# Five routing stages of a one-core transformer kernel: token numbers as two 16-bit digits, one row gather ahead of the stage barrier

## What is computed

```
layer 0: 8 experts, top 2, hidden 352 (and a shared expert)   weights = softmax over experts
layer 1: 8 experts, top 1, hidden 1024, biases
layer 2: two groups of 32 experts, top 2, hidden 128, added
layer 3: 32 experts, top 1, hidden 256, at most 80 tokens each (tokens past that are dropped)
ffn(x)[t] = sum over the chosen experts e of  w[t,e] * (silu(x[t] @ gate_e) * (x[t] @ up_e)) @ down_e
```

## Time and profile before

| | before |
|---|---|
| median of 3 runs | 2540.61 us (2532.79 to 2540.71) |
| the profiled execution | 2542.26 us, its span 2540.5 us |
| busy PE / PE weight load | 2044.3 us (80%) / 1660.4 us (65%) |
| busy DVE / ACT / POOL | 1307.0 us (51%) / 842.3 us (33%) / 737.2 us (29%) |
| granted TensorE clock, mean | 0.88 of full speed |
| DMA | 280.78 MB, mean 111 GB/s |

### The profile page before, as it was taken

How to read it: one execution, slowest core, us unless ns; L and a number is a source line. 1 busy time by engine, 2 the same in 40 slices (tenths; PEclk the granted TensorE clock), 3 DMA queues, 4 the chain that set the end, 5 groups by cost and what they waited for, 6 DMA issues and landing times. The chain is left out here.

```text
span 2540.5 us, 41393 instructions
## 1 busy us (share of the span) xinstructions
PE 2044.3 (80%) x13605; PEld 1660.4 (65%) x13605; DVE 1307.0 (51%) x3958; ACT 842.3 (33%) x2000; POOL 737.2 (29%) x928
## 2 busy tenths in 40 slices
PE   6869979992799999998589748995895953887694
PEld 5657746661698989987589735664684832554594
DVE  3532225524688888886400156765346445675423
ACT  4613313422133333333333223453341421345321
POOL 1022100005344444454111122310546743231132
PEclk9969989985899999999699969995796986898797
DMA  2052130002211111100199534426576653442384
GB/s 79 9 207 63 53 114 13 1 1 77 84 35 42 43 44 43 38 20 7 60 354 335 206 111 123 134 71 233 158 146 235 176 107 101 117 118 57 141 310 155
DMA packets 142732, 280.78 MB, mean 111 GB/s; under 512 B 20160, under 2 KB 99008, under 8 KB 138432
## 3 DMA queue, kind: packets, MB, share of 16 engines
q1 hardware_dynamic: 125824, 232.49, 27.3%
q0 software_dynamic: 16704, 45.64, 7.7%
HBM read 218.94 MB, written 56.62 MB: 108 GB/s over the span
## 5 line engine op out<-in xcount | busy, mean ns | idle before, releaser
L1956 PE MATMUL heads_ps_c<-heads_band,heads_sT 128*128 128x129 f32 x3072 | 368.9, 277 | 14.4 <-DVE heads_band L2175 13.4
L1956 PEld LDWEIGHTS heads_ps_c<-heads_band,heads_sT 128*128 128x128 f32 x3072 | 355.0, 192 | 24.7 <-issue 22.9
L2112 POOL TENSOR_SCALAR heads_band<-heads_shifts,heads_taps 128x130 f32<-128x130 f32 x384 | 251.1, 668 | 254.5 <-PE heads_ps_c L1956 250.3
L506 POOL DMA_INDIRECT weights_xg<-xn_rows,token_of x197 | 189.9, 964 | 449.3 <-DVE token_of L686 192.8
L2175 DVE SCALAR_TENSOR_TENSOR heads_band<-heads_shifts,heads_taps,heads_band 128x130 f32<-128x130 f32 x768 | 226.7, 351 | 18.4 <-POOL heads_band L2112 13.7
L2049 ACT ACTIVATE heads_probs<-heads_mixes,heads_least 128x256 f32<-128x256 f32 x256 | 116.1, 500 | 343.8 <-DVE heads_least L2188 343.8
L1697 DVE TENSOR_REDUCE heads_negmax<-heads_ps_m 128x2 f32<-128x512 f32 x256 | 169.6, 688 | 83.6 <-PE heads_ps_m L1553 81.3
L1654 ACT ACTIVATE heads_probsT<-heads_ps_e 128x512 f32<-128x512 f32 x256 | 147.1, 596 | 196.2 <-PE heads_ps_e L1577 195.8
L1032 PE MATMUL experts_ps_g<-weights_w,experts_xT 128*128 x504 | 135.0, 392 | 3.1 <-ACT experts_xT L1082 2.5
L1055 PE MATMUL experts_ps_y<-weights_w,experts_hT 128*128 (+1 forms) x486 | 133.6, 383 | 1.1 <-DVE experts_y L1117 1.1
L1167 POOL DMA_INDIRECT combine_yg<-y_rows,slot_of x48 | 45.4, 946 | 300.7 <-SPq L66 286.7
(11 more groups left out here) (386 smaller groups left out, 4245.4 us busy)
## 6 DMA issues: line engine op xcount, KB each, us to landing
experts_w<-in_experts_dram SPq DMA_DIRECT2D x23, 2180.0 KB, 10.0
weights_w<-in_experts_dram SPq DMA_DIRECT2D x16, 1536.0 KB
weights_w<-in_experts_dram SPq DMA_DIRECT2D x32, 768.0 KB, 6.4
piece_rows<-heads_pieces SPq DMA_DIRECT2D x96, 192.0 KB, 2.7
y_rows<-experts_y SPq DMA_DIRECT2D x125, 128.0 KB, 1.9
heads_stackQ<-piece_rows SPq DMA_DIRECT2D x48, 192.0 KB
heads_stackK<-piece_rows SPq DMA_DIRECT2D x48, 192.0 KB
weights_w<-in_experts_dram SPq DMA_DIRECT2D x8, 1088.0 KB
```

The costliest lines, as they stand in the source:

```text
L506: pool.indirect_dma_start(self.xg[:, u, :], None, xn_dram, bass.IndirectOffsetOnAxis(ap=tb.token_of[:, j:j + 1], axis=0)).then_inc(self.x_ ...
L1956: last = pe.matmul(out[:, qc * SEQ + k0:qc * SEQ + k1], sT[:, h % 2, kc, qc * P + dq:qc * P + dq + P], band[:, h % 2, dq, w0:w0 + k1 - k0] ...
L2112: last = pool.tensor_scalar(band[:, h % 2, dq, :], shifts[:, 0, :], taps[:, r % 2, h, dq * TAPS:dq * TAPS + 1], None, ALU.mult)
```

## The change

- Tokens as digits. Token = 128 x tile + lane. The one-hots, `hi` and `lo` become bf16, so that every value is at most 128 and exact. DVE writes only the two one-hots. ACT multiplies `tile_hot` by the lane number (one instruction a chunk, scale read per lane from `tb.column`) and by the tile number (one instruction with a constant for each tile of the chunk: 2 for K = 2, 4 for K = 1) into `digits`. PE's products have 2 x NT columns, bf16, and DVE puts the digits together behind them.
- The products with zeros go; the first and last product open and close the sum.
- `hot` is written tiles outermost, the order of its inputs; PE reads it with a stride instead.
- `FirstRows.COUNT` goes from 3 to 1; row tiles 1 and 2 are gathered at the start of the expert stage.
- In the load stage two index tables go and a bf16 one comes.

```diff
 class FirstRows:
-    COUNT = 3
+    COUNT = 1
...
-        hot = s.sb("hot", [P, E, TILES], BF16)
+        hot = s.sb("hot", [P, TILES, E], BF16)
...
-        lo, hi = s.sb("lo", [P, NK]), s.sb("hi", [P, NK])
-        lane_hot, tile_hot = s.sb("lane_hot", [P, 2, CH, P]), s.sb("tile_hot", [P, 2, CH, NT])
+        lo, hi = s.sb("lo", [P, NK], BF16), s.sb("hi", [P, NK], BF16)
+        lane_hot, tile_hot = s.sb("lane_hot", [P, 2, CH, P], BF16), s.sb("tile_hot", [P, 2, CH, NT], BF16)
+        digits = s.sb("digits", [P, 2, CH, 2, NT], BF16)
+        tokens = s.sb("tokens", [P, 1, NT])
...
             act.activation(ek[:, :, :], ek[:, :, :], ACT.Exp).then_inc(exped, 1)
+            for c in range(NK // CH):
+                act.wait_ge(tile_ready, c + 1)
+                if c >= 2:
+                    act.wait_ge(chunk_used, c - 1)
+                act.activation(digits[:, c % 2, :, 0, :], tile_hot[:, c % 2, :, :], ACT.Copy, scale=tb.column[:, 0:1])
+                for n in range(0, CH, K):
+                    last = act.activation(digits[:, c % 2, n:n + K, 1, :], tile_hot[:, c % 2, n:n + K, :], ACT.Copy,
+                                          scale=float((CH * c + n) // K))
+                last.then_inc(chunk_ready, 1)
...
-            out = ps_tok[:, 0:NT]
-            pe.matmul(out, ones[:, :], tb.zeros[:, 0:NT], start=True, stop=False, skip_group_check=True)
+            out = ps_tok[:, 0:2 * NT]
             pe.wait_ge(hot_ready, 1)
-            flat = hot[:, :, :].rearrange("p e t -> p (e t)")
+            flat = hot[:, :, :].rearrange("p t e -> p e t")
...
             for c in range(NK // CH):
+                pe.wait_ge(lane_ready, c + 1)
                 pe.wait_ge(chunk_ready, c + 1)
                 for n in range(CH):
-                    last = pe.matmul(out, lane_hot[:, c % 2, n, :], tile_hot[:, c % 2, n, :], start=False, stop=False,
-                                     skip_group_check=True)
+                    last = pe.matmul(out, lane_hot[:, c % 2, n, :], digits[:, c % 2, n, :, :].rearrange("p d n -> p (d n)"),
+                                     start=(c == n == 0), stop=(c == NK // CH - 1 and n == CH - 1))
                 last.then_inc(chunk_used, 1)
-            pe.matmul(out, ones[:, :], tb.zeros[:, 0:NT], start=False, stop=True, skip_group_check=True)\
-                .then_inc(summed, 1)
...
-                v.tensor_tensor(th, tb.row_iota[:, 0:NT].unsqueeze(1).to_broadcast([P, CH, NT]),
-                                hi[:, n].unsqueeze(2).to_broadcast([P, CH, NT]), ALU.is_equal).then_inc(own, 1)
-                steps.n += 1
-                v.tensor_tensor(lh, tb.row_iota[:, :].unsqueeze(1).to_broadcast([P, CH, P]),
-                                lo[:, n].unsqueeze(2).to_broadcast([P, CH, P]), ALU.is_equal)
-                v.wait_ge(own, steps.n)
-                v.tensor_tensor(th, th, tb.token_id[K][:, n].unsqueeze(2).to_broadcast([P, CH, NT]), ALU.mult)\
-                    .then_inc(chunk_ready, 1)
+                v.tensor_tensor(tile_hot[:, c % 2, :, :], tb.iota16[:, 0:NT].unsqueeze(1).to_broadcast([P, CH, NT]),
+                                hi[:, n].unsqueeze(2).to_broadcast([P, CH, NT]), ALU.is_equal).then_inc(tile_ready, 1)
+                v.tensor_tensor(lane_hot[:, c % 2, :, :], tb.iota16[:, :].unsqueeze(1).to_broadcast([P, CH, P]),
+                                lo[:, n].unsqueeze(2).to_broadcast([P, CH, P]), ALU.is_equal).then_inc(lane_ready, 1)
...
-            v.wait_ge(summed, 1)
-            v.tensor_copy(tb.token_of[:, 0:NT], ps_tok[:, 0:NT]).then_inc(token_ready, 1)
+            v.wait_ge(chunk_used, NK // CH)
+            steps.done(v.tensor_copy(tokens[:, 0, :], ps_tok[:, 0:NT]))
+            v.scalar_tensor_tensor(tb.token_of[:, 0:NT], ps_tok[:, NT:2 * NT], float(P), tokens[:, 0, :],
+                                   ALU.mult, ALU.add).then_inc(token_ready, 1)
```

More of the change, by code:

```diff
@@ L470, in __init__ @@
         self.restart = core.keep("restart", [P, 32 * TILES])
-        self.token_id = {1: core.keep("token_id1", [P, TILES]), 2: core.keep("token_id2", [P, TILES * 2])}
-        self.zeros = core.keep("zeros", [P, 64])
+        self.iota16, self.zeros16 = core.keep("iota16", [P, P], BF16), core.keep("zeros16", [P, P], BF16)
         self.token_of = core.keep("token_of", [P, most_tiles], U32)
@@ L537, in route_stage @@
         own, maxed, shifted, exped = s.sem("own"), s.sem("maxed"), s.sem("shifted"), s.sem("exped")
-        hot_ready, counted, placed, chunk_ready = (s.sem(n) for n in ("hot_ready", "counted", "placed", "chunk_ready"))
-        chunk_used, summed, token_ready = s.sem("chunk_used"), s.sem("summed"), s.sem("token_ready")
+        hot_ready, counted, placed, tile_ready, lane_ready, chunk_ready = (
+            s.sem(n) for n in ("hot_ready", "counted", "placed", "tile_ready", "lane_ready", "chunk_ready"))
+        chunk_used, token_ready = s.sem("chunk_used"), s.sem("token_ready")
         xn_stored, bias_loaded, gathered = s.sem("xn_stored"), s.sem("bias_loaded"), s.sem("gathered")
@@ L615, in _ @@
             if K == 2:
-                v.tensor_tensor(by_tile(hot[:, :, :]), hot_k[:, 0, :, :], hot_k[:, 1, :, :], ALU.add)\
+                v.tensor_tensor(hot[:, :, :], hot_k[:, 0, :, :], hot_k[:, 1, :, :], ALU.add)\
                     .then_inc(hot_ready, 1)
             else:
-                v.tensor_copy(by_tile(hot[:, :, :]), hot_k[:, 0, :, :]).then_inc(hot_ready, 1)
+                v.tensor_copy(hot[:, :, :], hot_k[:, 0, :, :]).then_inc(hot_ready, 1)
             v.wait_ge(exped, 2)
@@ L667, in _ @@
                 n = slice(CH * c, CH * (c + 1))
-                th, lh = tile_hot[:, c % 2, :, :], lane_hot[:, c % 2, :, :]
-                v.tensor_tensor(th, tb.row_iota[:, 0:NT].unsqueeze(1).to_broadcast([P, CH, NT]),
-                                hi[:, n].unsqueeze(2).to_broadcast([P, CH, NT]), ALU.is_equal).then_inc(own, 1)
-                steps.n += 1
-                v.tensor_tensor(lh, tb.row_iota[:, :].unsqueeze(1).to_broadcast([P, CH, P]),
-                                lo[:, n].unsqueeze(2).to_broadcast([P, CH, P]), ALU.is_equal)
-                v.wait_ge(own, steps.n)
-                v.tensor_tensor(th, th, tb.token_id[K][:, n].unsqueeze(2).to_broadcast([P, CH, NT]), ALU.mult)\
-                    .then_inc(chunk_ready, 1)
+                v.tensor_tensor(tile_hot[:, c % 2, :, :], tb.iota16[:, 0:NT].unsqueeze(1).to_broadcast([P, CH, NT]),
+                                hi[:, n].unsqueeze(2).to_broadcast([P, CH, NT]), ALU.is_equal).then_inc(tile_ready, 1)
+                v.tensor_tensor(lane_hot[:, c % 2, :, :], tb.iota16[:, :].unsqueeze(1).to_broadcast([P, CH, P]),
+                                lo[:, n].unsqueeze(2).to_broadcast([P, CH, P]), ALU.is_equal).then_inc(lane_ready, 1)
             if capacity is None:
@@ L2676, in _ @@
                 pool.memset(eps[:, :], LN_EPS)
-                pool.memset(tb.zeros[:, :], 0.0)
+                pool.memset(tb.zeros16[:, :], 0.0)
+                pool.iota(tb.iota16[:, :], [[1, P]], base=0, channel_multiplier=0,
+                          allow_small_or_imprecise_dtypes=True)
                 pool.iota(tb.row_iota[:, :], [[1, P]], base=0, channel_multiplier=0,
@@ L2681, in _ @@
                           allow_small_or_imprecise_dtypes=True)
-                for k in (1, 2):
-                    pool.iota(tb.token_id[k][:, :].rearrange("p (t k) -> p t k", k=k), [[P, TILES], [0, k]],
-                              base=0, channel_multiplier=1, allow_small_or_imprecise_dtypes=True)
                 pool.memset(tb.ones16[:, :], 1.0)
```

## The result

The changed kernel takes 2519.06 us (median of four runs, 2515.7 to 2521.6) where the kernel before takes 2540.66: a ratio of 0.992, 95% interval 0.9894 to 0.9946. The forecast was 2519. The profiled execution took 2516.72, span 2514.8. That the total agrees to the microsecond is luck: two stages gained more than forecast and two less, and in the profiled executions the five stages together gained 23.7 us where 21.1 were forecast, as the table shows.

What follows compares the result with a forecast made beforehand. Five stretches from routing to first hidden layer, where PE is not busy, bound the gain; shifts 3.8 + 6.2 + 5.0 + 1.9 + 4.2 and 0.2 at load make 21.3 us, so 2540.6 - 21.3 gives 2519, range 2507 to 2535.

Steps and rivals of the forecast that it cites:

- Inversion: Routing, first tile_hot to end of token_of: 9.95 us against 16.0 in the third routing, 6.0 saved.
- the ring of two buffers: Inversion: a buffer comes free once PE has used it, so two chunks cost one round of 2.17 us.
- One-hots priced as 32-bit: DVE's one-hots in the inversion gain nothing per instruction from bf16; otherwise 0.5 us less in a K = 2 stage.
- hot: Routing: writing it in order saves 1.6 us in each route2, 0.8 in route3, 0.4 in route0, 0.15 in route1.
- The barrier 3.1 behind POOL: Between routing and experts: PE starts 3.1 us after POOL ends.
- Row tile 1 late beside a load: Start of the expert stage: its gather lands after 8.0 us beside a load, 2.9 with a quiet DMA.
- Two tiles more behind the same stall: Experts of route2_0: row tile 1 replaces row tile 3 at PE's stall; two more tiles cost 3.2 us, leaving 5.0 gained.
- route1: Its first hidden layer: 4.15 + 2.5 = 6.65 us earlier at the barrier, 0.45 lost to two more gathers, 6.2 gained.
- Row tile 1 not late: Rival, start of the expert stages: gathers land in 2.9 us even beside a load; 29.6 us saved, 2511; chance 0.12.
- inversion as long as before: Rival, routing: ACT's chain takes the place of PE's, 1.7 us a chunk; 4.8 us saved, 2536; chance 0.15.
- Very late: Rival, PE's wait before hidden layer 0: row tile 1 lands after 12.4 us in every stage; 6.9 us slower, 2547; chance 0.07.

Runs made afterwards that it cites:

- e4: Changed kernel with COUNT = 3 and the old order of hot, so only the two-digit inversion is left: 2524.96 us, ratio 0.9936 to the kernel before.
- e7: Changed kernel with four chunk buffers instead of two in the route2 stages; trace only: token_of ended 9.1 us after the first tile_hot.
- e5: Changed kernel with COUNT = 0, no gather in front of the barrier: ratio 0.9910 to the kernel before.
- e6: Changed kernel, but in experts2_0 SP starts loading the experts2_1 weights only once 8 row tiles are turned: ratio 0.9957 to the kernel before.
- e8: Changed kernel with the weights experts2_0 fetches ahead issued in 8 pieces, one behind every fourth store: ratio 0.9937 to the kernel before.
- e1_count3: Changed kernel with COUNT put back to 3, the rest kept: 2523.06 us, ratio 0.9935 to the kernel before.
- e2: Kernel before with COUNT = 1 and nothing else: 2537.82 us, ratio 0.9986 to the kernel before.

## Why the prediction was right or wrong, step by step

- **Inversion: right.** First `tile_hot` to the end of `token_of`: in the profile after, 9.9 and 10.0 in the `route2` stages (9.95 forecast), 8.1 in `route0` (8.4), 4.4 in `route1` (4.7), 4.75 in `route3` (4.9). `e4` shows that it carries 21.4 of the gain, `e7` that the ring of two buffers is its pace, as in the sum.
- **One-hots priced as 32-bit: right.** `lane_hot` takes 0.68 in bf16 where it took 0.69, `tile_hot` 0.42 as before. The Trainium skill's rule (VectorE: DVE Perf Modes, What auto-detection actually checks) that an operand without unit step forbids the faster mode fits these rows. What made the inversion shorter is PE's part: 0.58 us a chunk for 1.74, both at a granted clock of 0.50.
- **`hot`: mis-sized.** 1.3 in a `route2` stage, not 1.6. I took the difference of durations; what counts is from start to next start. It is 3.0 in all for 4.5. That PE's strided read (1.02 us for 0.61) would be covered was right.
- **The barrier 3.1 behind POOL: the step that failed.** It waits for the landing of what POOL has issued: POOL's drain lasts until then, and `e5` shows that without a gather the wait is gone. In the earlier trace rows the last gather landed in 2.8 us, so both readings give the same 3.1. Where the DMA is full, the barrier of `route0` moved 7.3 instead of 10.2, and that of `route3` 4.6 instead of 7.2; this is why `route3` gave 2.8 and not 4.2 (some of the 2.6 came back, since its first hidden layer stood 4.3 behind the barrier and not 4.9). In `route0` it cost nothing, since row tile 1 landed in 4.4 instead of my 7, at the end of the load. In `route2_0` the barrier moved 10.1, not 8.15: I had DVE's tail end it both times, with 3.5 us between the earlier trace rows. But DVE needs 0.8, and the 3.5 was the landing of POOL's third gather.
- **Row tile 1 late beside a load: right in size and cause.** 7.4 us of landing (8.0 forecast), and `e6` and `e8` take it away with the load. In `route2_1`, without a load, PE waited 3.3 for it (3.2 landing, 2.9 forecast).
- **Two tiles more behind the same stall, 3.2 us: mis-sized, and it left out the clock.** `route2_0` gained 8.1, not 5.0. Most of the difference is the barrier, 2.0 earlier than forecast. The stall behind it also ended 0.5 sooner (8.2 us behind the barrier, where it was 8.7 for row tile 3 before). The two tiles then cost 5.0 instead of 3.2: row tiles 2 and 3 follow at 2.67 and 2.33, at a granted clock of 0.50 (1.2 GHz). But the kernel before pays the same price one step later. Row tile 4 follows row tile 3 only after 3.75 us, where later turns follow at 1.63. That is no second stall for a gather: PE is idle for 0.42 of it and then busy, and L1032 takes 2.02 where it takes 1.03 at full clock. The rows of `before`, with two windows in the form of the earlier trace rows (PE's busy time and count stand first, the granted clock third from the end), and then the same two turns of `e1_count3`:

```profile
1804.43 2.02 PE L1032 MATMUL experts_ps_g<-weights_w,experts_xT 128*128 x4 [0.42 <-ACT experts_xT L1082]
1807.32 0.63 PE L1021 MATMUL experts_ps_x<-ident,weights_xg 128*128 128x128 f32 x2
...
1809.46 1.03 PE L1032 MATMUL experts_ps_g<-weights_w,experts_xT 128*128 x4
...
1805.00:1806.00 1.00, 1.00 (x4) 0.82 (x3) 0.00 (x0) 0.00 (x0) 0.70 (x2) 0.50 1.04 343
...
1809.00:1812.00 3.00, 3.00 (x18) 2.50 (x18) 1.32 (x4) 1.52 (x6) 1.59 (x3) 1.00 0.57 184
```

```profile
1784.75 0.44 PE L1027 MATMUL experts_ps_x<-ident,weights_xg 128*128 128x128 f32 x2 [2.08 <-DMA weights_xg<-xn_rows,token_of]
1788.15 0.63 PE L1027 MATMUL experts_ps_x<-ident,weights_xg 128*128 128x128 f32 x2
```

  That is 3.40 us in `e1`. In `before` PE had been busy without a gap from 1798 to 1801, its granted clock was 0.98 from 1801 to 1803.5, and after the stall (idle 2.37) it was 0.50 again from 1805 to 1807.5. With `COUNT` at 1 PE is past this stretch when it turns row tile 4, 1.63 behind row tile 3. The sum is 10.1 + 0.5 - 5.0 + (3.75 - 1.63) = 7.7 of the 8.1.
- **`route1`: right up to 1.5.** Theory and `e2` agree on 2.5 at the barrier. But the first weights also came 9.9 us behind it instead of 12.3; in all kernels with `COUNT` at 1 here it is 9.7 to 10.1, and in the four with 3 it is 11.9 to 12.3. The first hidden layer was thus 9.4 earlier, and a later wait for weights took 1.7 back. Why they land earlier is not settled.
- **The range and the rivals.** 2519.06 is inside. "Row tile 1 not late" failed on the 7.5 us stall, "inversion as long as before" on 9.9 us. "Very late" did not occur: 13.0 is still the latest landing of all, but not of a row tile 1.

## What to carry to other kernels

A barrier behind an indirect DMA is as late as its landing, not its issue: count it from the landing, and put a gather in front only if something else ends later anyway (in `route2_1`, behind POOL's late gathers, three in front were better than one). Choose such a number by stage, since one number for all hid +2.9 and -2.8. And before you remove a wait, ask what else happens under it: 4 us of earlier rows came to nothing here, because another stall, whose cause is open, lay beneath.

## What the runs showed of the hardware

- The landing of one gather of 128 rows: 2.7 to 3.2 us with a quiet DMA, 5.8 to 6.1 with a DMA share of 1.0 at some 420 GB/s, 7.4 beside a load that starts with it, 7.1 behind POOL's late gathers.
- The end of a block waits for the landing of the indirect DMAs that POOL has issued: its drain took 6.5 and 6.1 us with one gather in flight under a full DMA, and 0.04 us with none.
- PE reads 512 bf16 columns that lie 64 bytes apart in 1.02 us, and the same columns in order in 0.61, both at a granted clock of 0.50.
- After a stall of 2.37 us PE's granted clock was 0.50 for a while, though PE was busy throughout: the four products of L1032 took 2.02 us there, and 1.03 a little later at 1.00.
- The Trainium skill (SBUF — State Buffer, Who interferes with whom) says that a DVE instruction with two SBUF inputs contends with a GpSimd one that reads SBUF. This trace agrees: a POOL gather of 0.95 took 2.25 and 1.85 where DVE's long two-input instruction (L694, 2.25) began beside it, and 1.11 in `route0`, where that instruction takes 0.47.
